# Gated attention: the low half of the output projection's weights subtracted on GpSimd, in pieces, in place of VectorE

## What is computed

```python
ln_out = _ln(hidden_states, ln_w, ln_b)
q  = _ln(_fp8_linear_pertensor(ln_out, wq, ...))        # 8 groups x 2 heads x 128
k  = _ln(_fp8_linear_pertensor(ln_out, wk, ...)); v = _fp8_linear_pertensor(ln_out, wv, ...)
core = _gqa(q, k, v)
qx = _ln(_fp8_linear_pertensor(ln_out, wqx, ...)); kx, vx = split(cond @ w_kv_x)
xout = _gqa(qx, _ln(kx), vx)
catq = _div_clamp_fp8(concatenate([core, xout]), proj_smooth)
return einsum('bsi,oi->bso', catq, wproj) * (proj_in_scale * proj_w_scale)
```

## Time and profile before

| what | us |
|---|---|
| three runs: median (lowest, highest) | 1005.81 (1003.88, 1030.69) |
| the profiled execution, its own time | 1006.87 |
| its span, first to last instruction | 1005.1 |
| busy: PE / DVE / ACT / POOL | 891.5 / 721.0 / 567.5 / 298.8 |
| attention stage, from the start to about | 452 |
| one period (two steps, one group) | 49.3 |

### The profile page before, as it was taken

The page is one execution under the profiler, slowest core; times in us unless marked ns, Lnnn a source line. Parts: engine busy times, 40 slices in busy tenths (PEclk is TensorE's granted clock), DMA queues, the critical chain, the costliest instruction groups (busy, mean ns, idle before and its releaser), DMA issues. The chain is left out here.

```text
span 1005.1 us, 18511 instructions
## 1 busy us (share of the span) xinstructions
PE 891.5 (89%) x6876; PEld 725.0 (72%) x6878; DVE 721.0 (72%) x1203; ACT 567.5 (56%) x1715; POOL 298.8 (30%) x454
## 2 busy tenths in 40 slices
PE   1678999999999999977999999997899997899997
PEld 1667888888888888864777777774555554677776
DVE  7878898989898988796564444446658787666653
ACT  5677878778787877732543333323457774233332
POOL 1133434343333333423322222203113233242320
PEclk9989999999999999978999999998569997999999
DMA  4101010101010100006011111001000000101001
GB/s 150 43 1 64 2 64 1 65 2 65 1 64 2 64 2 23 1 1 248 14 40 48 51 50 50 3 0 63 1 2 1 2 2 32 63 32 50 13 0 43
DMA packets 10929, 35.74 MB, mean 36 GB/s; under 512 B 1248, under 2 KB 5344, under 8 KB 8544
## 3 DMA queue, kind: packets, MB, share of 16 engines
q1 hardware_dynamic: 10704, 34.64, 9.7%
q10 hardware_dynamic: 144, 0.03, 0.0%
HBM read 33.62 MB, written 1.05 MB: 34 GB/s over the span
## 5 line engine op out<-in xcount | busy, mean ns | idle before, releaser
L236 PE MATMUL ps<-wt_hi,xq 128*128 128x256 f32 (+1 forms) x512 | 124.4, 279 | 20.3 <-DVE ctx_lo L824 14.7
L236 PE MATMUL ps<-wt_lo,xq 128*128 128x256 f32 (+1 forms) x512 | 123.9, 283 | 0.0
L236 PEld LDWEIGHTS ps<-wt_hi,xq 128*128 128x128 f32 x512 | 100.2, 196 | 23.1 <-DVE ctx_lo L824 15.1
L414 ACT ACTIVATE square<-ps 128x128 bf16<-128x128 f32 x384 | 100.9, 295 | 26.6 <-PE ps L236 26.5
L236 PEld LDWEIGHTS ps<-wt_lo,xq 128*128 128x128 f32 x512 | 99.9, 195 | 0.0
L1247 POOL TENSOR_TENSOR moe_w_lo<-moe_w_all,moe_w_hi 128x384 fp32r<-128x384 f32 x48 | 53.5, 1149 | 133.3 <-ACT moe_w_hi L1350 133.3
L1683 ACT ACTIVATE ca_probs<-ps 128x512 f32<-128x512 f32 x128 | 69.5, 594 | 38.3 <-PE ps L1612 37.5
L572 POOL TENSOR_TENSOR rstd<-rstd,half_neg 128x6 f32<-128x6 f32 x64 | 88.3, 1380 | 5.0
L414 ACT ACTIVATION_READ_ACCUMULATOR square<-ps 128x1 f32 x384 | 85.9, 227 | 0.0
L1764 DVE TENSOR_REDUCE context_mx<-ps 128x4 f32<-128x1024 f32 x64 | 76.4, 1213 | 10.2 <-PE ps L1586 10.0
L1419 DVE TENSOR_TENSOR moe_act_g<-moe_act_g,ps 128x512 f32<-128x512 f32 x48 | 33.1, 689 | 67.5 <-PE ps L1284 67.5
(11 more groups left out here) (219 smaller groups left out, 2616.9 us busy)
## 6 DMA issues: line engine op xcount, KB each, us to landing
moe_w_all<-in_experts SPq DMA_DIRECT2D x8, 1152.0 KB, 5.2
w_in<-in_wt SPq DMA_DIRECT2D x8, 1024.0 KB, 5.8
wp_in<-in_wp SPq DMA_DIRECT2D x8, 512.0 KB, 3.6
ffn_codes<-in_codes SPq DMA_DIRECT2D x8, 384.0 KB, 3.1
ffn_w_scales<-in_code_scales SPq DMA_DIRECT2D x8, 384.0 KB, 3.7
x_rows<-in_x SPq DMA_DIRECT2D x2, 512.0 KB, 4.7
ctx_in<-in_ctxT SPq DMA_DIRECT2D x1, 1024.0 KB, 9.0
context_rows<-in_ctx SPq DMA_DIRECT2D x1, 1024.0 KB, 8.9
```

The source lines that it names most:

```text
L236: last = mm(ps[:, first + bank, col:col + width], left[:, c, tokens], w[:, c, wcol:wcol + width], start=(j == 0), stop=(j == len(steps) - 1))
L414: last = nc.scalar.activation(square[:, i % 2, j, :], ps[:, bank, (j % 4) * P:(j % 4) * P + P], ACT.Square, scale=float(HD) ** -0.5, accum ...
```

## The change

VectorE's `output_weights_low`, which wrote the whole of `wp_lo` (128x1024) in one instruction in the odd step, is gone. A function of the same name on GpSimd writes it in four pieces of 128x256 in the even step that follows: piece 0 between the first two `rstd_of`, piece 1 behind them, pieces 2 and 3 behind `normalise_probs(h - 1, 0)`. The semaphore `wp_lo_done` is raised behind the last piece. The last group stays where it was. SyncE, TensorE and ScalarE keep their programs.

```diff
+            def output_weights_low(g, parts):
+                if 0 in parts:
+                    pool.wait_ge(s["wp_hi_done"], g + 1)
+                for f in parts:
+                    last = nc.gpsimd.tensor_tensor(wp_lo[:, f, :], wp_in[:, f, :], wp_hi[:, f, :].bitcast(F32), ALU.subtract)
+                if 2 * HPG - 1 in parts:
+                    last.then_inc(s["wp_lo_done"], 1)
+
             def step(h):
-                g, here = h // 2, is_unit(h)
-                if here:
-                    rstd_of(h, 0)
-                    rstd_of(h, 1)
+                g = h // 2 - 1
+                low = h % 2 == 0 and g >= 0
+                rstd_of(h, 0)
+                if low:
+                    output_weights_low(g, (0,))
+                rstd_of(h, 1)
+                if low:
+                    output_weights_low(g, (1,))
                 if is_unit(h - 1):
                     normalise_probs(h - 1, 0)
-                if here:
-                    rstd_of(h, 2)
-                    rstd_of(h, 3)
+                if low:
+                    output_weights_low(g, (2, 3))
+                rstd_of(h, 2)
+                rstd_of(h, 3)
                 if is_unit(h - 1):
                     normalise_probs(h - 1, 1)
 
             def tail():
-                g = GROUPS - 1
-                pool.wait_ge(s["wp_hi_done"], g + 1)
-                for f in range(2 * HPG):
-                    last = nc.gpsimd.tensor_tensor(wp_lo[:, f, :], wp_in[:, f, :], wp_hi[:, f, :].bitcast(F32), ALU.subtract)
-                last.then_inc(s["wp_lo_done"], 1)
+                output_weights_low(GROUPS - 1, range(2 * HPG))
...
-            def output_weights_low(g):
-                dve.wait_ge(s["wp_hi_done"], g + 1)
-                nc.vector.tensor_tensor(wp_lo[:].rearrange("p f o -> p (f o)"), wp_in[:].rearrange("p f o -> p (f o)"),
-                                        wp_hi[:].rearrange("p f o -> p (f o)").bitcast(F32), ALU.subtract).then_inc(s["wp_lo_done"], 1)
-
...
-                if h % 2 == 1 and h < LAST:
-                    output_weights_low(g)
```

## The result

| | before | after |
|---|---|---|
| median of the runs, us (lowest, highest; 4 runs each) | 1006.55 (1003.88, 1030.69) | 1071.15 (1070.33, 1072.21) |
| ratio | | 1.0652, 95% interval 1.0625 to 1.0678 |
| the profiled execution / its span, us | 1006.87 / 1005.1 | 1070.33 / 1068.2 |
| end of the attention stage (first load of the next one issued) | 453.02 | 522.59 |
| one period | 49.32 | 60.83 (mean of five, 59.60 to 61.87) |

The changed kernel is 6.5% slower; the forecast was 1074 us, 6.7%. (In the changed file the lines of this stage stand up to nine further down: `w_mean` is line 639, not 630, the second half of `qn` 670, not 666, `wp_lo` on GpSimd 584.)

A forecast was written before the change was run, and what follows sets the result against it. It saw no single bound: four engines pass work around a loop, each a few tenths of a us behind the next. 6 x (9.0 + 2.2 + 0) = 67 us on 1006.9 gives 1074 us, 6.7% slower; range 1046 to 1094 us.

The forecast's parts named there:

- stall of `sum_weights`: VectorE's sum_weights waits for the w_in load held up in SyncE's queue: 9.0 us, six times.
- clock behind the gap: TensorE restarts at half clock after 9.4 us without a matmul, losing 2.2 us each time (ends 0 and 4.4).
- relief of VectorE against contention: VectorE's removed subtractions (credit 0 to 0.5 us a period) against GpSimd's added pieces: about zero, -0.5 to +1.1.
- The landing term: Time from issue of the w_in load on SyncE until it has landed: 5.8 us at the median, 5.6 to 7.9.
- part is absorbed: Rival: VectorE's 5.1 us of idle time a period works off part of the stall; 1044 us, chance 0.09.
- the two old gaps of 4.38 us: TensorE gaps before 53.13 and 469.26 in the old trace; clock fell to 0.50, staying 5.0 and 5.2 us after restart.
- The rivals without it (1061 us): Rival: stall on TensorE without the clock's price, 6 x 9.0 = 54 us; 1061 us, chance 0.14.
- dearer (1092 us): Rival: slower load landing, pieces 2 and 3 at 1.71 us, or longer half clock; 1092 us, chance 0.13.
- I carry 0: Net of VectorE's credit and GpSimd's piece costs taken as 0 a period, with ends -0.5 and +1.1 us.
- the contention of piece 0: GpSimd's piece 0 between the two rstd costs at most 0.3 us uncontended, 1.1 if it takes 1.71.
- The other side: Rival, not slower: w_in is not held up and VectorE's relief of 14.2 us counts; 993 us, chance 0.04.
- Everything after this stage unchanged: Expected sign in the profile after: stages behind the attention stage stay as they were.

The follow-up runs named there:

- e3: The changed kernel with nine identity matmuls on TensorE before outputs in the six stalling even steps; 1054.88 us, ratio 1.0507.
- e4: The kernel before, subtraction still on VectorE, but the w_in load of groups 2 to 7 waits for probs of the even step; 1052.70 us, ratio 1.0462.
- e5: The changed kernel with pieces 2 and 3 ahead of probs instead of behind it, loads in the old order; 1055.03 us, ratio 1.0482.
- e1: The changed kernel with SyncE issuing w_in of the next group ahead of the wp_in that waits for wp_lo; 1010.47 us, ratio 1.0054.
- e2: The kernel before with the same swapped order of loads as e1; 1003.45 us against 1003.66, ratio 1.000.
- e8: The changed kernel with swapped loads, pieces 2 and 3 ahead of probs, and take(h-1, 0) ahead of the wp_hi cast; 1002.26 us, ratio 0.9967.
- e6: e1 with ScalarE's take(h-1, 0) moved ahead of the cast that makes wp_hi in odd steps; 1006.53 us, ratio 1.0014.
- e7: e5 (pieces 2 and 3 ahead of probs) with the swapped loads of e1; 1007.72 us, ratio 1.0021.

## Why the prediction was right

The mechanism was there as put; that the total came within 3 us is in part luck, since the stage lost 2.6 us more than forecast and the channel attention gave back 6.0 that no term held. Link by link: SyncE issues `w_in` 0.37 us behind `wp_in`, the reduction waits, ScalarE and TensorE stand behind it, six times, in the even steps. By terms, per period:

| term | forecast | measured | from |
|---|---|---|---|
| stall of `sum_weights` | 9.0 | 9.3 | waits of the kernel after |
| clock behind the gap | 2.2 | 1.8 (e3); 2.3 left over in e4, e5 | e3, e4, e5 |
| relief of VectorE against contention | 0 (-0.5 to +1.1) | +0.4 with the stall (left over), +0.87 without | e3; e1 |
| period | 60.5 | 60.8 | loads of the kernel after |
| attention stage in all | +67 | +69.6 | stage ends |

- *The stall.* The landing term was taken at 5.8 us, and the six loads take 5.5 to 7.7, 6.1 at the median. e3, e4 and e5 show that the stall goes onto the path whole: no later wait took any of it up, as argued. The rival "part is absorbed" (1044 us) falls with that.
- *The clock.* The rows behind the two old gaps of 4.38 us gave the right size, a little high: 5.1 us at half clock were taken, and the six restarts have 3.4 to 6.1, 4.4 on average. At 0.44 us lost for each that is 1.9 us, beside the 1.8 of e3. The rivals without it (1061 us) and dearer (1092 us) fall with e3.
- *The relief.* VectorE's 14.2 us turned into waiting, as forecast: its waits for ScalarE's `scaled` went from 8.0 us (7 times, whole stage) to 20.7 (14 times). The step "I carry 0" was near enough for the changed kernel (0.4 us) only because the stall itself kept VectorE idle beside pieces 2 and 3. I had priced the contention of piece 0, which met none (0.72 us), and missed two others: the addition for `rstd`, which the last instruction of a `quantise` that moved up runs into (1.07 us in the changed kernel as well), and pieces 2 and 3 once nothing stalls. That, and not the order of loads, is what makes e1 slower than the kernel before: seven groups at 0.87 are 6.1 of the 6.7 us by which its stage is longer than e2's.
- *The other side* (993 us) has its test in e1: with the load issued in time the kernel is not faster, 0.5% slower. And in e8, with pieces 2 and 3 out of VectorE's way and the addition down to 0.62 us, a period is only 0.11 us shorter than before, of the 2.03 us that VectorE was relieved of. So the relief is worth next to nothing where four engines hand on to each other with hardly any lead.
- "Everything after this stage unchanged" was wrong by 6 us, in the kernel's favour. Without it the profiled execution would have taken 1076 us and not 1070.

## What to carry to other kernels

Before work is moved to another engine, follow the semaphore it raises: here it also released a transfer, and behind that transfer, in the same in-order queue, stood the one that mattered. When a wait is added or made later, list what stands behind the waiting instruction in its queue, and put what has its own condition met in front of it (e1: 60 of 65 us back by exchanging two lines). And an idle engine is no sign of room: what counts is whether the moved instruction runs beside one of another engine that slows it or that it slows (a 0.20 us addition took 1.07), and whether its result comes before or behind the hand-over.

## What the runs showed of the hardware that I had not expected

**GpSimd and VectorE appear to take turns, not to share.** Where GpSimd's addition meets VectorE's `catq`, an instruction with two SBUF inputs, its end follows the end of that instruction and not its own start. In e1 the addition starts at 235.95, VectorE's `catq` ends at 236.95, the addition at 237.02. In the kernel after it is 208.13, 209.14 and 209.20, in e8 185.28, 185.85 and 185.90. The addition takes 0.20 us by itself. In the other direction VectorE's L97, with one input, waits for GpSimd: in e1 GpSimd's pieces end at 246.69, and L97 ends at 246.97 after 0.96 us. In the tail of the kernel before, the fourth piece outlasts VectorE's update by 0.6 us (430.5 against 429.89), close to its own length of 0.7. The Trainium skill (GPSIMD Engine Reference, "Key points") names the contention; these rows suggest its form (read from ends that coincide, not tested by itself): the later one waits, so a tiny instruction on the path can lose 0.9 us to one that it merely touches. One row does not fit a plain taking of turns. The power that starts at 185.52 in the kernel before takes 1.77 us, 0.45 more than alone, and ends at 187.29 while `catq` runs beside it from 186.15 to 187.37 at its usual 1.22. So what exactly excludes what is open.

**A later stage runs at one of two mean clocks.** The channel attention is the same code in all kernels, with the same 1263 matmuls. Its length goes with its granted clock: besides the two rows above, e2 and e8 read

```profile
686.50:839.20 152.70, 134.89 (x1263) 79.89 (x1264) 114.16 (x172) 90.97 (x166) 48.52 (x178) 0.82 0.03 12
```

```profile
690.80:838.30 147.50, 127.08 (x1263) 75.76 (x1264) 114.10 (x172) 91.01 (x166) 50.15 (x178) 0.88 0.04 12
```

It takes 152.5 to 153.2 us at 0.82 or 0.83 in the kernel before, e1, e2, e5, e6 and e7, and 147.2 to 147.5 us at 0.87 or 0.88 in the kernel after, e3 and e8, at equal ScalarE work; nothing lies between (the longest execution of e4, at 165.0 us and 0.76, stands apart). So 5 to 6 us of a total can come from there. Whether a change decides it, by moving the stage in time, or chance does is not shown: there is one trace of each kernel, and the kernel before by itself took from 1000 to 1008 us in 29 runs. It means that differences of half a per cent in this kernel are better read from the periods in the trace than from the total.

**A load lands faster alone.** 1 MB of `w_in` takes 5.5 to 7.9 us behind 0.5 MB of `wp_in` issued 0.37 us ahead (kernels before and after), and 4.7 to 4.9 us alone (e4); in e1, where no `wp_in` is in flight beside it either, 4.7 to 5.1.
